# A graph attention layer on one core: first two key groups handled pair by pair in 64-row array mode, with halved transposes and masks

## What is computed

```python
q = (x_norm @ Wq + bq).reshape(N, H, HD)
k = (x_norm @ Wk + bk).reshape(N, H, HD)
v = (x_norm @ Wv + bv).reshape(N, H, HD)
scores = jnp.einsum('ehd,ehd->eh', q[origin], k[destination]) * SCALE
ws = scores * edge_weights
seg_max = jax.ops.segment_max(ws, origin, num_segments=N)
e = jnp.exp(ws - seg_max[origin])
denom = jax.ops.segment_sum(e, origin, num_segments=N)
att = e / (denom[origin] + 1e-16)
values = jax.ops.segment_sum(att[:, :, None] * v[destination], origin, num_segments=N)
```

## Time and profile before

| | |
|---|---|
| median of 3 runs | 1079.44 us (1079.01 to 1079.73) |
| the profiled execution | 1079.38 us |
| its span, first to last instruction | 1077.5 us |
| PE busy over the span | 737.6 us (68%) |
| DVE busy | 544.0 us (50%) |
| ScalarE (ACT) busy | 397.4 us (37%) |
| attention stage in the trace | 673 to about 1048 us, then a short end |

### The profile page before, as it was taken

How to read it: one execution, slowest core, us unless ns; L and a number is a source line. 1 busy time by engine, 2 the same in 40 slices (tenths; PEclk the granted TensorE clock), 3 DMA queues, 4 the chain that set the end, 5 groups by cost and what they waited for, 6 DMA issues and landing times.

```text
span 1077.5 us, 13741 instructions
## 1 busy us (share of the span) xinstructions
PE 737.6 (68%) x4498; PEld 436.4 (41%) x4537; DVE 544.0 (50%) x1269; ACT 397.4 (37%) x943; POOL 392.7 (36%) x401
## 2 busy tenths in 40 slices
PE   7744510494332211115999999999999999999996
PEld 4321100241001011003544454576766667767773
DVE  4601400482000110200532473888889999999998
ACT  2300001020000000001313020689989998877773
POOL 2677577477777776562572000000000000000002
PEclk9956655696555555556999999999999999999998
DMA  9788866536500000002400021444444444443323
GB/s 323 270 292 302 281 239 212 179 112 219 193 23 3 23 3 22 22 3 79 153 2 1 1 79 78 149 185 172 158 157 157 161 164 167 150 140 137 137 69 96
DMA packets 71115, 143.12 MB, mean 133 GB/s; under 512 B 22565, under 2 KB 57137, under 8 KB 67079
## 3 DMA queue, kind: packets, MB, share of 16 engines
q1 hardware_dynamic: 48884, 120.06, 30.7%
q10 hardware_dynamic: 8464, 15.84, 4.2%
q0 software_dynamic: 13696, 6.33, 3.1%
HBM read 77.47 MB, written 64.80 MB: 132 GB/s over the span
## 4 chain that ended last, share of the span: by engine, by line
PE 50%; another core or an unknown queue 20%; issue 20%; DVE 6%; ACT 2%; DMA 2%; ACTq 1%; DVEq 0%; POOLq 0%
PE bank L1092 11%; PE bank L1319 9%; PE bank L1364 7%; PE bank L1342 7%; PE bank L1077 6%; PE bank L1388 3%; PE bank L1326 2%; DVE AR L1841 1%; PE bank L1370 1%; DMA AR<-in_L_mix_bp_dram 1%; DVE QMN L1451 1%; DVE QMN L1450 1%; PE bank L1112 1%; DMA AR<-kv_rows,xd 1%
## 5 line engine op out<-in xcount | busy, mean ns | idle before, releaser
L630 POOL DMA_INDIRECT w_tab<-pay,idx x330 | 326.5, 989 | 160.0 <-issue 116.1
L1077 PE MATMUL bank<-AR 128*128 128x512 f32 (+1 forms) x288 | 130.9, 587 | 122.7 <-issue 102.8
L705 POOL DMA_INDIRECT AR<-kv_rows,xd x10 | 10.5, 1051 | 445.4 <-PE bank L1364 331.6
L1092 PE MATMUL bank<-AR 128*128 128x512 f32 (+1 forms) x240 | 128.6, 666 | 62.4 <-issue 62.4
L1077 PEld LDWEIGHTS bank<-AR 128*128 128x128 f32 x288 | 62.3, 222 | 180.3 <-issue 156.3
L1541 DVE TENSOR_TENSOR V<-bank,bias_row 128x512 f32<-128x512 f32 (+1 forms) x10 | 6.9, 691 | 250.0 <-remote 153.5
L912 ACT ACTIVATE AR<-AR,nmx 128x512 f32<-128x512 f32 (+1 forms) x180 | 118.5, 662 | 20.6 <-DVE nmx L1855 20.5
L1841 DVE CUSTOM_DVE_ANT_0 AR<-bank,AR,MX 128x512 f32<-128x512 f32 (+1 forms) x120 | 114.9, 986 | 8.6 <-remote 7.6
L1319 PE MATMUL bank<-KT,QT 64*128 64x512 f32 (+1 forms) x480 | 108.6, 568 | 4.0 <-ACT bank L920 3.7
L1092 PEld LDWEIGHTS bank<-AR 128*128 128x128 f32 (+1 forms) x240 | 48.3, 205 | 133.5 <-issue 133.0
L1364 PE MATMUL bank<-AR,V 128*64 128x128 f32 (+1 forms) x1520 | 101.9, 274 | 0.2 <-ACT AR L927 0.2
(11 more groups left out here) (272 smaller groups left out, 1013.2 us busy)
## 6 DMA issues: line engine op xcount, KB each, us to landing
w_tab<-ztile SPq DMA_DIRECT2D x20, 2280.0 KB
AR<-w_tab SPq DMA_DIRECT2D x20, 2048.0 KB, 7.4
AR<-w_tab SPq DMA_DIRECT2D x10, 1344.0 KB, 6.2
w_tab<-ztile SPq DMA_DIRECT2D x3, 1800.0 KB
w_tab<-pay,idx POOLq DMA_INDIRECT x330
w_tab<-ztile SPq DMA_DIRECT2D x2, 1700.0 KB
kv_rows<-AR ACTq DMA_DIRECT2D x9, 256.0 KB
kv_rows<-V ACTq DMA_DIRECT2D x9, 256.0 KB
```

What stands on the lines that cost most here:

```text
L630: pool.indirect_dma_start(out=w_tab, out_offset=bass.IndirectOffsetOnAxis(ap=idx[:, k, j:j + 1], axis=0), in_=pay[:, k % RING, j, :], in_o ...
L1077: last = mm(b[:, 0:n], w[:, k, m * P:(m + 1) * P], src_t(k), start=(k == 0), stop=(k == KC - 1))
L1092: last = mm(b[0:r, :], src_t(k)[:, 0:r], w[:, k, :], start=(k == 0), stop=(k == KC - 1))
```

## The change

For rounds 0 to 19, PE handles one pair after the other (`pair_step`): scores of pair u, first halves of its masks, first halves of the transposes of the pair two before, second halves of the masks, second halves of the transposes. Masks and transposes are now matmuls of 64 array rows; in the first half head 0 takes rows 0 to 63 and head 1 rows 64 to 127, in the second half the other way round. Since two row halves add into the same bank, PE waits for its own semaphores (`s_mh`, `s_th`) before the second halves. Only pair 2 is laid by ScalarE, both heads, after the exps of pair 0; before, pair 2, head 1 of pair 1 and head 1 of pair 3 were. ScalarE also takes the copy of head 1 of pair 0 from DVE. DVE changes signs right after each pair's two products, and rescales after the products of pair 3. The bank uses are put in the new order. Round 20 and later keep their order.

```diff
-ODD_ON_ACT = ((2,), (1, 2), ())
-OVER_MASK = (((3, 1), (1, 1), (2, 0), (2, 1)), ((3, 1), (1, 1), (2, 0), (2, 1)), ((2, 0), (2, 1), (3, 1), (0, 0), (1, 0)))
+ODD_ON_ACT = ((0, 2), (0, 1, 2), ())
+OVER_MASK = (((2, 0), (2, 1)), ((2, 0), (2, 1)), ((2, 0), (2, 1), (3, 1), (0, 0), (1, 0)))
...
+def paired(d):
+
+    return d < 4 * NT
+
+
+def half(j, n):
+
+    return slice(64 * j, min(64 * j + 64, n))
...
+    if paired(_d):
+        USES += [("s", 2 * _d, 0), ("s", 2 * _d, 1)]
+        if _q == 1 and NT <= _w - 1:
+            USES += [("f", _w - 1)]
+        if _d:
+            USES += [("t", 2 * _d - 2, 0), ("t", 2 * _d - 2, 1)]
+        USES += [("s", 2 * _d + 1, 0), ("s", 2 * _d + 1, 1)]
+        if _q == 1 and _w + 1 == 2 * NT:
+            USES += [("l", _w + 1)]
+        if _d:
+            USES += [("t", 2 * _d - 1, 0), ("t", 2 * _d - 1, 1)]
+        continue
...
+                if paired(d):
+                    if d:
                         pairs(2 * d - 2)
-                    if NT <= w - 1:
+                    if q == 0 and NT <= w - 1:
                         change(w - 1)
-                    if 2 <= w <= NT + 1:
+                    if q == 0 and 2 <= w <= NT + 1:
                         keep(w - 2)
-                    if d >= 1 and not late:
-                        pairs(2 * d - 2)
+                    exps(2 * d)
+                    if q == 0:
+                        for u, hh in lay_order(d):
+                            lay_mask(u, hh)
...
+            def turn_halves(u, part):
...
+                for i, (a, rws, _) in enumerate(bl):
+                    for hh in range(2):
+                        rows = half((hh + part) % 2, r)
+                        last = mm(use(("t", u, hh))[0:rws, i * P + rows.start:i * P + rows.stop], ws[g][u % 4][hh][rows, a:a + rws], ident[rows, rows],
+                                  start=(part == 0 and i == 0), stop=(part == 1 and i == len(bl) - 1), is_transpose=True)
...
+            def pair_step(d, i):
...
+                pair_scores(u)
+                mask_half(u, 0)
+                if fac:
+                    factor_half(w - 1, 0)
+                if los:
+                    loser_half(w + 1, 0)
+                if d:
+                    turn_halves(older, 0)
+                mask_half(u, 1)
+                pe.wait_ge(s_th, th.n)
...
+                if paired(d):
+                    if q == 0 and NT <= w - 1:
+                        change(w - 1)
+                    if q == 0 and NT <= w - 2:
+                        merged(w - 2)
+                    weighted(2 * d, 0)
+                    weighted(2 * d, 1)
+                    early = q == 1 and w + 1 == 2 * NT
+                    if early:
+                        rescaled(w - 1)
+                    if d:
+                        odd_of(2 * d - 2)
+                    shift_of(2 * d)
+                    weighted(2 * d + 1, 0)
+                    weighted(2 * d + 1, 1)
+                    if q == 1 and NT <= w - 1 and not early:
+                        rescaled(w - 1)
+                    shift_of(2 * d + 1)
+                    if q == 1:
+                        mask(w + 1)
```

More of the change, by code:

```diff
@@ L1326, in scores, with pair_scores @@
                         mm(use(("s", u, hh))[:, 0:n], identb[:, :], pen[w % 2][:, 0:n], start=False, stop=True).then_inc(s_s[i], 1)
+            mh, th = Count(pe, s_mh), Count(pe, s_th)
+            def pair_scores(u):
+                w, p = u // 4, u % 4
+                g, c = w // NT, w % NT
+                d0, n = GROUPS[g]
+                over = [laid(u, hh) for hh in range(2)]
+                if u in (1, 2):
+                    banks_left((2 * u - 2, 2 * u - 1))
+                for hh in range(2):
+                    if over[hh]:
+                        pe.wait_ge(s_laid, LAID_OF[u, hh] + 1)
+                    else:
+                        free(pe, ("s", u, hh))
+                for hh in range(2):
+                    last = mm(use(("s", u, hh))[:, 0:n], QT[64 * hh:64 * hh + 64, p, c * P:(c + 1) * P], KT[64 * hh:64 * hh + 64, p, d0:d0 + n],
+                              start=not over[hh], stop=over[hh], skip_group_check=over[hh])
+                    if over[hh]:
+                        last.then_inc(s_s[2 * (u % 2) + hh], 1)
@@ new lines, in mask_half @@
+            def mask_half(u, part):
+                w, n = u // 4, GROUPS[u // 4 // NT][1]
+                bare = [hh for hh in range(2) if not laid(u, hh)]
+                if bare and part:
+                    pe.wait_ge(s_mh, mh.n)
+                elif bare:
+                    pe.wait_ge(s_pen, w + 1)
+                for hh in bare:
+                    rows = half((hh + part) % 2, P)
+                    last = mm(use(("s", u, hh))[:, 0:n], identb[rows, :], pen[w % 2][rows, 0:n], start=False, stop=(part == 1))
+                    if part:
+                        last.then_inc(s_s[2 * (u % 2) + hh], 1)
+                    else:
+                        mh.inc(last)
@@ new lines, in factor_half @@
+            def factor_half(w, part):
+                if part == 0:
+                    pe.wait_ge(s_fo, w - NT + 1)
+                    free(pe, ("f", w))
+                rows = half(part, P)
+                for p in range(KC):
+                    last = mm(use(("f", w))[:, p * P + rows.start:p * P + rows.stop], fo[rows, p * P:(p + 1) * P], ident[rows, rows],
+                              start=(part == 0 and p == 0), stop=(part == 1 and p == KC - 1), is_transpose=True)
+                if part:
+                    last.then_inc(s_fp, 1)
+                else:
+                    th.inc(last)
@@ new lines, in loser_half @@
+            def loser_half(w, part):
+                c = w - 2 * NT
+                if part == 0:
+                    pe.wait_ge(s_kvx[c % 3], 16 * (c // 3 + 1))
+                    free(pe, ("l", w))
+                rows = half(part, X)
+                for k in range(KC):
+                    last = mm(use(("l", w))[:, k * X + rows.start:k * X + rows.stop], KVx[c % 3][rows, k * P:(k + 1) * P], ident[rows, rows],
+                              start=(part == 0 and k == 0), stop=(part == 1 and k == KC - 1), is_transpose=True)
+                if part:
+                    last.then_inc(s_kxp, 1)
+                else:
+                    th.inc(last)
@@ L1407, in _ @@
                     inverse(w - 2)
-                if q == 1 and NT <= w - 1 < NW:
+                if q == 1 and NT <= w - 1 < NW and not paired(d):
                     factor(w - 1)
```

65 lines of the change are left out of this document (51 added, 14 removed).

## The result

The changed kernel takes 1103.09 us (median of 4 runs, 1100.25 to 1104.52) against 1079.22 for the kernel before on the same chip: a ratio of 1.0224, with a 95% interval of 1.0195 to 1.0253. It is slower, as forecast; it takes more than the 1096 us forecast and lies inside the range. The profiled execution took 1100.25 us with a span of 1098.3, so 20.8 us more than the span before. From DVE's first product to the first product of round 20 it is 948.7 - 675.4 = 273.3 us instead of 927.4 - 675.5 = 251.9, and nothing else changed but 0.6 us in rounds 20 and later.

What follows compares the result with a forecast made beforehand. PE, DVE and ScalarE are nearly full, so the waits between them decide. Losses by round, mainly +10.8 us in rounds 10 to 18, sum to +16.6 on the profiled 1079.38: 1096 us, range 1084 to 1111.

Steps and rivals of the forecast that it cites:

- even step, first group: Rounds 0 to 9, DVE's first product of pair 0 to that of pair 2: 6.2 to 6.3 us, before 5.24.
- odd step, first group: Rounds 0 to 9, DVE's first product of pair 2 to that of the next pair 0: 6.3 us.
- even step, second group: Rounds 10 to 19, pair 0 to pair 2 on DVE, with products 1.08 apart: 6.4 us.
- odd step, second group: Rounds 10 to 19, pair 2 to next pair 0 on DVE, with PE waiting for the rescale: 7.8 us.
- self waits that were small: PE's waits on its own results, possibly priced too low: +1 us in the sum.
- The lays are on the path: Even step: PE waits for ScalarE's lays of pair 2 behind pair 0's exps; the step gets 1.0 us longer.
- The factor's bank is waited for: Second group's odd step: next pair 0 needs the factor's bank until the rescale; PE ready about a microsecond earlier.
- PE has about 11.2 us of work: PE's own work a round with the change, about 11.2 us instead of 12.2.
- rival 1: Half transposes do not pay, a set takes 0.44 us: 1111 us; at 0.084 a block, 1103; chance 0.10.
- The half set is 0.23: On PE, one set of half transposes, 4 blocks of both heads, takes 0.23 us at 0.058 a block.
- Rival 2 (PE stays the bound): Lays end before PE's values, so only PE's list counts: -18 us, 1061 us; chance 0.06.
- pair 3 reaches DVE at 2.8: Second group's odd step: pair 3 reaches DVE 2.8 us after pair 2's product began.

Runs made afterwards that it cites:

- e1: Changed kernel with ScalarE laying both masks of pair 2 ahead of the exps of pair 0: 716.69 us on another chip, 1.0085 of the kernel before.
- e7: Changed kernel with no lays in rounds 0 to 19, PE masking pair 2 too: 724.23 us on another chip, 1.0196 of the kernel before.
- e3: Kernel before with pair 2's two lays behind the exps of pair 0 in rounds 0 to 19: 762.50 us on another chip, ratio 1.0710.
- e2: Changed kernel with DVE's rescale behind pair 2's products, not pair 3's, in the second group: 726.94 us on another chip, 1.0211 of the kernel before.
- e6: Changed kernel with lays ahead of the exps and rescale behind pair 2's products: 711.87 us on another chip, 1.0011 of the kernel before.
- e11: Changed kernel with whole 128-row masks at the place of the first halves, transposes still halved: 725.47 us on another chip, 1.0205 of the kernel before.
- e4: Changed kernel with full 128-row transposes at the second halves' place, the factor's still halved: 749.96 us on another chip, 1.0528 of the kernel before.
- e9: Changed kernel with the first pair's sign change back behind the second pair's first product: 760.55 us on another chip, 1.0681 of the kernel before.

## Why the prediction held, and where its sizes were off

| part | said | measured |
|---|---|---|
| even step, first group | 6.2 to 6.3 | 6.33 |
| odd step, first group | 6.3 | 6.43 |
| even step, second group | 6.4 | 6.49 |
| odd step, second group | 7.8 | 8.09 |
| round 0 | +1.5 | 12.94 - 11.06 = +1.9 |
| rounds 1 to 9 | +1.8 | +3.7 |
| rounds 10 to 18 | +10.8 | +12.4 |
| round 19 | +2.2 | 16.0 - 12.55 = +3.45 |
| round 20 | -0.7 | 9.89 - 10.42 = -0.5 |
| self waits that were small | +1 | part of the above |

*The lays are on the path* held in both directions and in both kernels (e1, e7, e3), in the change to 0.1 us. *The factor's bank is waited for* held: e2 took that wait away, and e6 showed that it adds to the other. *PE has about 11.2 us of work*: 11.5 or a little more. With the lays out of the way (e1) a first-group round takes 11.79, and PE is busy for 131.7 of 135 us.

The measured 1103 us is also what the forecast gave for its half of rival 1 (a block every 0.084 us), and that is a coincidence: the blocks did not come so slowly, and the difference stands elsewhere. *The half set is 0.23*: it is 0.26 (751.65 to 751.91), the pitch per pair of records 0.056 to 0.062, so rival 1's mechanism did not come. Nor did the Trainium skill's rule (TensorE: Matmul & The Clock Gate, LDWEIGHTS: a load takes columns / 1.2 ns) show: these loads have 128 columns too, and two of them start every 0.06 us.

*Rival 2 (PE stays the bound)* stated the point from which it decides: the way through exps and lays a microsecond shorter. e1 made it so, and the first group came down from 12.4 to 11.8, half of the way to the 11.2 that this rival gave.

The step that was mis-sized in the second group is "pair 3 reaches DVE at 2.8". It was 3.22. I had let the transposes of pair 1 start when PE was there, and looked only at the factor's own bank in the instruction order; the factor also shifts every use behind it by one bank, which puts pair 1's transposes behind the second product of pair 2. Pair 3's second mask halves stand behind these transposes in PE's list, so DVE gets pair 3 later too. e11 took pair 3's masks out from behind the wait, and pair 3 came 0.72 us sooner. In the first group no single step failed: the two steps are 0.1 longer each, and over nine rounds that makes most of the second 1.9 us. For the even step the mechanism was exact and the addition was not: the listed terms add up to 6.33, which is what was measured, and not to 6.2 to 6.3. For the odd step, mask build to DVE's product took 1.05 us (751.42 to 752.47) where the terms gave 0.95: the transposes between the mask halves 0.26 for 0.23, and 0.56 from the second mask half to DVE for 0.50. Round 19 and round 0 were guesses between bounds; round 19 lies above its own. There PE stood 1.40 us on round 20's first lay (its scores at 947.42), behind two exps again: the same mechanism as in the even step, which I had not looked for at the seam.

## What to carry to other kernels

When work is moved to an engine that is often idle, ask where in its list the piece stands, not how idle it is: 1.1 us of lays behind an engine's critical operation cost 1.0 us a round, and with the same lays ahead of it no wait on them was left. In a rotation of buffers, inserting one use moves every later use to another buffer: walk the whole ring, and note for each use whose reader it now waits for. When a view names a releaser that had long been done, or none, look for the operation that ended just before the wait did. And judge the parts of a change apart: the half transposes here saved some 1.5 us a round of PE's time (an estimate from e4), and two misplaced list entries hid it.

## What the runs showed that was not expected

PE's granted clock also falls inside a loop that otherwise has it at 1.00. In e3 and e9, rounds 0 to 19 have 27 waits of PE of 1.90 to 2.8 us; in 17 of these rounds the granted clock was 0.87 to 0.90, and where a like round at 1.00 stands near, the round was 0.9 to 1.7 us longer. Shorter waits had it seldom: one of the nine waits of 1.82 us in e9's first group was followed by it (round 1, clock 0.89, 15.24 us instead of 13.7), and none of the waits of up to 1.42 us in the change. So a wait can be dearer than its length, and whether it is does not follow from its length alone.

The wait of a matmul on its own engine's result, for the second row half of the same bank, is 0.35 us uncovered (masks in e4: 0.79 us for two halves that take 0.22 each) and close to nothing when another pair of heads' half transposes stand in it (the change: 0.26 us from the first transposes to the second mask half, which is what the transposes take themselves).
